# Layer norms whose tiles are turned one by one, with late low parts and a late Newton start

## The reference

```
x = conv block L0 (pooled attention over 64 keys, batch norm, residual)
x = conv block L1 (binary 3x3 and 1x1 convolutions, PReLU)
t = tokens(x)                                    # (8, 256, 64)
t = t + attention_8_heads(layer_norm(t))
t = t + mixture_of_8_experts(layer_norm(t))      # softmax gate, top 2, GELU
t = t + haar_attention(layer_norm(t))
t = t + mixture_of_16_experts(layer_norm(t))     # softmax gate, top 2, SiLU
layer_norm(v) = (v - mean(v)) / sqrt(var(v) + 1e-5), over the 64 channels
```

## Time and profile before

| what | value |
|---|---|
| runs, median (lowest to highest) | 419.47 us (419.42 to 420.14) |
| the profiled execution's own time | 416.06 us |
| its span | 414.3 us |
| its mean granted clock | 0.897 |
| busy: TensorE, VectorE, ScalarE, GpSimd | 350.9, 283.2, 217.5, 189.2 us |

### The profile page before, as it was taken

The page is one execution under the profiler, slowest core; times in us unless marked ns, Lnnn a source line. Parts: engine busy times, 40 slices in busy tenths (PEclk is TensorE's granted clock), DMA queues, the critical chain, the costliest instruction groups (busy, mean ns, idle before and its releaser), DMA issues.

```text
span 414.3 us, 6910 instructions
## 1 busy us (share of the span) xinstructions
PE 350.9 (85%) x2145; PEld 246.1 (59%) x2147; DVE 283.2 (68%) x689; ACT 217.5 (52%) x541; POOL 189.2 (46%) x186
## 2 busy tenths in 40 slices
PE   5666259999999999999769699877258999999996
PEld 1552156787888878887467244374147756666662
DVE  2767876788878878877493587579798545555441
ACT  0534258677677767778547435261315634444441
POOL 4120025545454545545315800122110299999994
PEclk9867559999999999999977789968556999999999
DMA  6916000000000000000000795000000576666521
GB/s 185 235 21 205 0 0 1 2 2 2 2 0 0 0 0 0 0 0 2 1 2 5 288 329 197 2 0 2 1 0 2 193 273 215 222 208 224 204 101 52
DMA packets 17002, 32.87 MB, mean 79 GB/s; under 512 B 6032, under 2 KB 9808, under 8 KB 16976
## 3 DMA queue, kind: packets, MB, share of 16 engines
q1 hardware_dynamic: 16976, 32.55, 23.9%
HBM read 31.83 MB, written 0.72 MB: 79 GB/s over the span
## 4 chain that ended last, share of the span: by engine, by line
PE 61%; DVE 19%; ACT 9%; issue 6%; DMA 3%; POOL 1%; SPq 0%; DVEq 0%; ACTq 0%; POOLq 0%
PE ps L1020 14%; PE ps L1028 7%; PE ps L857 6%; PE ps L884 5%; PE ps L868 5%; PE ps L976 4%; ACT va_vb L619 4%; DVE ln L1504 2%; DVE negmax L1574 2%; PE ps L968 2%; PE ps L807 2%; DMA pT<-gates_row 1%; PE ps L910 1%; PE ps L834 1%; PE ps L833 1%
## 5 line engine op out<-in xcount | busy, mean ns | idle before, releaser
L504 POOL TENSOR_TENSOR va_vb<-va_vb,rowinv 128x512 f32<-128x512 f32 x64 | 67.2, 1050 | 72.1 <-DVE rowinv L1581 72.1
L619 ACT ACTIVATE va_vb<-ps,negmax 128x256 f32<-128x256 f32 x128 | 59.5, 472 | 11.2 <-DVE negmax L1574 10.9
L1020 PE MATMUL ps<-XS,w3hl 128*128 128x512 f32 x256 | 63.4, 406 | 0.7 <-ACT gT L590 0.7
L733 ACT ACTIVATE wy<-ps 128x512 f32<-128x512 f32 x64 | 38.2, 598 | 45.6 <-PE ps L1020 45.6
L1020 PEld LDWEIGHTS ps<-XS,w3hl 128*128 128x128 f32 x256 | 48.6, 193 | 17.2 <-issue 4.9
L1574 DVE TENSOR_REDUCE negmax<-ps 128x2 f32<-128x512 f32 x64 | 44.0, 688 | 7.8 <-PE ps L857 5.6
L857 PE MATMUL ps<-keys_gates,xcur 128*128 128x256 f32 x256 | 47.4, 308 | 2.2 <-DVE keys_gates L1566 2.2
L857 PEld LDWEIGHTS ps<-keys_gates,xcur 128*128 128x128 f32 x256 | 35.1, 193 | 14.8 <-issue 11.5
L868 PE MATMUL ps<-consts,va_vb 128*128 128x128 f32 x256 | 39.5, 277 | 4.2 <-POOL va_vb L504 2.4
L462 POOL TENSOR_TENSOR xn<-T,lnc 128x512 f32<-128x512 f32 x4 | 4.2, 1042 | 74.0 <-DVE lnc L1512 74.0
L868 PEld LDWEIGHTS ps<-consts,va_vb 128*128 128x128 f32 x256 | 29.7, 147 | 9.8 <-POOL va_vb L504 4.8
(11 more groups left out here) (323 smaller groups left out, 727.9 us busy)
## 6 DMA issues: line engine op xcount, KB each, us to landing
pT<-gates_row SPq DMA_DIRECT2D x18, 512.0 KB, 4.8
vproj<-gates_row SPq DMA_DIRECT2D x16, 512.0 KB, 5.4
gate_row_keys<-gates_row SPq DMA_DIRECT2D x14, 512.0 KB, 4.9
early<-in_f_in SPq DMA_DIRECT2D x1, 2048.0 KB, 8.8
consts<-in_consts SPq DMA_DIRECT2D x1, 816.0 KB, 4.9
x<-in_x SPq DMA_DIRECT2D x1, 512.0 KB, 3.7
w2raw<-in_f_in SPq DMA_DIRECT2D x1, 512.0 KB, 3.5
out<-in_f_out SPq DMA_DIRECT2D x1, 512.0 KB
```

Source lines behind the costliest of these rows:

```text
L504: gp.tensor_tensor(prob[:, n % 4], prob[:, n % 4], rowinv[:, n % 4, :].unsqueeze(2).broadcast_to([P, U, N]), ALU.mult).then_inc(S("p_scale ...
L619: ins = act.activation(prob[:, n % 4, u, :], ps[:, 1 + n % 2, u * N:(u + 1) * N], ACT.Exp, bias=negmax[:, n % 4, u:u + 1], accum_out=rowsu ...
L733: act.activation(act_out[:, kk % 2, :], ps[:, 2 * (kk % 3), :], ACT.Silu).then_inc(S("f3_act"), 1)
L1020: mm = pe.matmul(ps[:, 2 * (kk % 3) + w, :], w3hl[:, s, e, w * HID:(w + 1) * HID], XS[:, c * CHUNK:(c + 1) * CHUNK], start=(s == 0), stop= ...
```

## The change

Per chunk there are four transposes of one tile each (64 columns of weights), all into rows 0 to 63 of one bank; one ScalarE copy of 64x512 puts the high part in the upper rows and one VectorE subtraction of 64x512 the low part in the lower. For norm 0 the chunks use banks 0, 5, 4 and 6, which the attention's first steps leave free for a while. In norm 0 VectorE makes only the first chunk's low part and the token copy, then the Newton start and the weight split, and the other three low parts in the attention steps -2, -1 and 0; TensorE waits for the split in step -1 and for the low parts in steps 0 and 1. Both halves of T are copied by ScalarE in norms 0 and 2, and VectorE takes the statistics of the first eight tiles as soon as the first half is there. In the gate the subtraction goes ahead of the comparison and writes to the tile that the exponential then works on in place.

```diff
--- before.py
+++ after.py
@@ -362,25 +362,22 @@
         block = ctx.enter_context(nc.Block())
 
 
+        def norm_bank(n, p):
+
+            return (0, 5, 4, 6)[p] if n == 0 else p
+
+        def chunk_of(stack, p):
+            return stack[:, p * CHUNK:(p + 1) * CHUNK]
+
         def split_high(act, stack, bank, p, signal):
 
-            for odd in range(2):
-                h = slice(C * odd, C * odd + C)
-                act.activation(tiles_of(stack, p, odd)[h], ps[h, bank, 0:2 * P].rearrange("p (t n) -> p t n", n=P),
-                               ACT.Copy).then_inc(S(signal), 1)
+            act.activation(chunk_of(stack, p)[0:C], ps[0:C, bank, :], ACT.Copy).then_inc(S(signal), 1)
 
         def split_low(dve, stack, bank, p, high, so_far, signal):
 
-            for odd in range(2):
-                h, o = slice(C * odd, C * odd + C), slice(C * (1 - odd), C * (1 - odd) + C)
-                dve.wait_ge(S(high), so_far + 2 * p + odd + 1)
-                ins = dve.tensor_tensor(tiles_of(stack, p, odd)[o], ps[h, bank, 0:2 * P].rearrange("p (t n) -> p t n", n=P),
-                                        tiles_of(stack, p, odd)[h].bitcast(F32), ALU.subtract)
-            ins.then_inc(S(signal), 1)
-
-        def tiles_of(stack, p, odd):
-
-            return stack[:, p * CHUNK:(p + 1) * CHUNK].rearrange("p (t o n) -> p t o n", o=2, n=P)[:, :, odd, :]
+            dve.wait_ge(S(high), so_far + p + 1)
+            dve.tensor_tensor(chunk_of(stack, p)[C:P], ps[0:C, bank, :], chunk_of(stack, p)[0:C].bitcast(F32),
+                              ALU.subtract).then_inc(S(signal), 1)
 
         @block.sync
         def _(sp):
@@ -576,12 +573,12 @@
                 act.preload_act_table(table_after)
             for p in range(4):
                 act.wait_ge(S("ln_transposed"), 4 * n + p + 1)
-                split_high(act, XS, p, p, "ln_high")
+                split_high(act, XS, norm_bank(n, p), p, "ln_high")
 
         def gate_act(act, n, first_chunks):
             experts = (EXP2, EXP3)[n]
             act.wait_ge(S("gate_shifted"), n + 1)
-            act.activation(gexp[:, :, 0:experts], logit[:, :, 0:experts],
+            act.activation(gexp[:, :, 0:experts], gexp[:, :, 0:experts],
                            ACT.Exp).then_inc(S("gate_exp"), 1)
             act.preload_act_table((ACT.Gelu, ACT.Silu)[n])
             first_chunks()
@@ -708,9 +705,10 @@
                                ACT.Identity, bias=col[:, 37:38]).then_inc(S("r1_shifted"), 1)
             for p in range(2):
                 positive(p, 2)
-            act.wait_ge(S("x2_transposed"), 1)
-            act.activation(T[:, 0:8, :].rearrange("p t c -> p (t c)"), ps[:, 4, :],
-                           ACT.Copy).then_inc(S("T_act"), 1)
+            for half in range(2):
+                act.wait_ge(S("x2_transposed"), half + 1)
+                act.activation(T[:, 8 * half:8 * half + 8, :].rearrange("p t c -> p (t c)"), ps[:, 4 + half, :],
+                               ACT.Copy).then_inc(S("T_act"), 1)
             ln_act(act, 0, ACT.Exp)
 
             attention_act(act)
@@ -739,8 +737,9 @@
                 gelu(kk)
             act.wait_ge(S("f2_out_chunk"), CHUNKS * EXP2 - 2)
             act.activation(sums[:, 0, :], ps[:, 6, :], ACT.Copy).then_inc(S("f2_sum_act"), 1)
-            act.wait_ge(S("f2_turned"), 1)
-            act.activation(stream_half(0), turned_half(0), ACT.Copy).then_inc(S("T_act"), 2)
+            for half in range(2):
+                act.wait_ge(S("f2_turned"), half + 1)
+                act.activation(stream_half(half), turned_half(half), ACT.Copy).then_inc(S("T_act"), 1)
             ln_act(act, 2)
 
             for half in range(2):
@@ -789,10 +788,8 @@
 
             for p in range(4):
                 pe.wait_ge(S("ln_normalised"), 4 * n + p + 1)
-                for t in range(2):
-                    q = CT * p + 2 * t
-                    mm = pe.transpose(ps[:, p, t * P:(t + 1) * P],
-                                      xn[:, q:q + 2].rearrange("p t c -> p (t c)"), ident)
+                for t in range(CT):
+                    mm = pe.transpose(ps[0:C, norm_bank(n, p), t * P:(t + 1) * P], xn[:, CT * p + t, :], ident)
                 mm.then_inc(S("ln_transposed"), 1)
 
         def gate_pe(pe, n):
@@ -921,6 +918,10 @@
                     keys(j, k + 2)
                 if in_loop:
                     newton_a()
+                if not in_loop and k == -1:
+                    pe.wait_ge(S("qkvw_ready"), 4)
+                if not in_loop and k in (0, 1):
+                    pe.wait_ge(S("ln_low"), k + 3)
                 if there(k):
                     turn(j, 2 * k)
                 if there(k + 1):
@@ -942,7 +943,6 @@
                     products(j, k - 1)
 
             pe.wait_ge(S("fold_split"), 3)
-            pe.wait_ge(S("nsx_ready"), 2)
             pe.sem_inc(S("pv_done"), PAIRS)
             pe.sem_inc(S("out_turned"), G)
             attention_steps(pe, step)
@@ -1472,16 +1472,16 @@
                 dve.wait_ge(S("r1_shifted"), p + 1)
                 norm_and_prelu(p, 2, "conv1_ready", 1, x2, "a2", "b23", "x2_ready")
 
-            dve.wait_ge(S("consts_loaded"), 16)
-            for d in range(2):
-                ins = dve.tensor_copy(eyedup[:, d * C:(d + 1) * C], ident[0:C, 0:C])
-            step(ins)
-            dve.wait_ge(S("ns_norm_done"), 1)
-            step(dve.reciprocal(nsc[:, 1:2], ps[:, 7, C:C + 1]))
-            ts(nsX[:, 2, :], nsAT[:, 0, :], nsc[:, 1:2], None, ALU.mult).then_inc(S("nsx_ready"), 1)
-            ts(nsX[:, 0:2, :], nsA[:].unsqueeze(1).broadcast_to([P, 2, C]), nsc[:, 1:2], None,
-               ALU.mult).then_inc(S("nsx_ready"), 1)
-
+            def newton_start():
+                dve.wait_ge(S("consts_loaded"), 16)
+                for d in range(2):
+                    ins = dve.tensor_copy(eyedup[:, d * C:(d + 1) * C], ident[0:C, 0:C])
+                step(ins)
+                dve.wait_ge(S("ns_norm_done"), 1)
+                step(dve.reciprocal(nsc[:, 1:2], ps[:, 7, C:C + 1]))
+                ts(nsX[:, 2, :], nsAT[:, 0, :], nsc[:, 1:2], None, ALU.mult).then_inc(S("nsx_ready"), 1)
+                ts(nsX[:, 0:2, :], nsA[:].unsqueeze(1).broadcast_to([P, 2, C]), nsc[:, 1:2], None,
+                   ALU.mult).then_inc(S("nsx_ready"), 1)
 
             def query_or_key(part, h):
                 return qkvw[:, part, 0:P].rearrange("p (a h c) -> p a h c", a=2, h=2)[:, :, h, :]
@@ -1493,14 +1493,12 @@
                                        (qkvw[:, 0, P:192], qkvw[:, 1, P:192], ps[:, 7, 0:C])):
                     step(dve.tensor_copy(high, raw))
                     tt(low, raw, high.bitcast(F32), ALU.subtract).then_inc(S("qkvw_ready"), 2)
-            split_projections()
-            dve.wait_ge(S("x2_transposed"), 2)
-            step(dve.tensor_copy(T[:, 8:16, :].rearrange("p t c -> p (t c)"), ps[:, 5, :]))
-            dve.wait_ge(S("T_act"), 1)
 
             def layer_norm(n, after_first=None):
 
                 for q in range(TILES):
+                    if n % 2 == 0 and q % 8 == 0:
+                        dve.wait_ge(S("T_act"), n + q // 8 + 1)
                     ins = dve.bn_stats(ln6[:, q, :], T[:, q, :])
                 step(ins)
 
@@ -1520,10 +1518,15 @@
                     if p == 2:
                         dve.wait_ge(S("ln_centred"), n + 1)
                     tt(xn[:, q], xn[:, q], wide(lnc[:, 7, q], t=CT), ALU.mult).then_inc(S("ln_normalised"), 1)
-                for p in range(4):
-                    split_low(dve, XS, p, p, "ln_high", 8 * n, "ln_low")
-                    if p == 0 and after_first:
-                        after_first()
+                if after_first:
+                    low(n, 0)
+                    after_first()
+                else:
+                    for p in range(4):
+                        low(n, p)
+
+            def low(n, p):
+                split_low(dve, XS, norm_bank(n, p), p, "ln_high", 4 * n, "ln_low")
 
             def gate(n):
 
@@ -1538,8 +1541,8 @@
                     for q in range(8 * half, 8 * half + 8):
                         ins = dve.max(top8[:, q, :], lg[:, q, :])
                 step(ins)
+                tt(ge, lg, wide(top8[:, :, 0], experts), ALU.subtract).then_inc(S("gate_shifted"), 1)
                 step(tt(gs, lg, wide(top8[:, :, 1], experts), ALU.is_ge))
-                tt(lg, lg, wide(top8[:, :, 0], experts), ALU.subtract).then_inc(S("gate_shifted"), 1)
                 dve.wait_ge(S("gate_exp"), n + 1)
                 step(tt(gs, ge, gs, ALU.mult))
 
@@ -1559,7 +1562,12 @@
                 dve.tensor_copy(xcur[:, m % 2, :].rearrange("p (u n) -> p u n", u=U).unsqueeze(1),
                                 src[:, at, :, m % 2, :]).then_inc(S("xcur_ready"), 1)
 
-            layer_norm(0, after_first=lambda: tokens(0, 0))
+            def while_first_keys():
+                tokens(0, 0)
+                newton_start()
+                split_projections()
+
```

(6 more changed lines are left out.)

## The result

| what | before | after |
|---|---|---|
| median of the runs | 419.45 us (416.30 to 420.14, 4 runs) | 413.03 us (412.62 to 413.48, 4 runs) |
| profiled execution, span | 416.06, 414.3 | 413.05, 411.2 |
| mean granted clock | 0.897 | 0.913 |
| busy TensorE, VectorE, ScalarE, GpSimd | 350.9, 283.2, 217.5, 189.2 | 349.5, 278.7, 214.6, 188.5 |

The ratio is 0.9874 (95% interval 0.9834 to 0.9914). Ratios and intervals use only the runs within 1.5% of the fastest run of the same kernel; medians are of all runs. The two profiled executions differ by 3.0 only. These are two questions: why 3.0 and not 2.1, and why the medians differ by twice what the traces do.

What follows compares the result with a forecast made beforehand. It took serial engine hand-overs in the four norms and a final GpSimd queue as the bound. Gains of 0.6 + 0.27 + 0.85 + 0.40 = 2.1 us gave a median of 417.4 us, range 415.4 to 419.0.

Steps and rivals of the forecast that it cites:

- the sum against the traced execution: Whole kernel: gains of 2.1 us taken off the profiled execution of 416.06, giving 413.96.
- the carry from that execution to the median: Whole kernel: the profiled execution's 3.4 us under the median was carried over in microseconds, giving a median of 417.4.
- Norm 0's entry: Start of norm 0: ScalarE's second copy of T and the later Newton start and split end the statistics 1.63 us sooner.
- the first rival: Norm 0: VectorE does not wait for GpSimd's bias adds; norm 0 gives 1.33, median 416.6 us, chance 0.20.
- the value taken: Norm 0, before the keys' low part: the identity copy hangs on GpSimd's adds; low part at 57.2, gain 1.3 us.
- its lower end: Norm 0, same place: the token copy also loses to GpSimd's second add; block ends at 57.4, gain 1.05 us.
- the bound of 0.42: Norm 0, first chunk: four 64-column transposes cost at most 0.42 us more than two of 128; 0.2 was taken.
- The 0.67 for the late low parts: First attention steps: chunk 2's low part costs 0.47 us and chunk 3's 0.20, with chunk 1's free.
- with no gap at half clock: Behind norms 1 and 2: gate matmuls (3.60 us) and projections (6.56) run unbroken at half clock, so later low-part savings give nothing.
- a rival at 0.10: TensorE's granted clock: less idling and more transposes delay its fall, saving 1.35 us at the projections; median 416.0, chance 0.10.
- the last stage is a GpSimd queue: Last stage: GpSimd's 64 products of 1.28 us, 82 in all, set the end, so bringing gate 1 forward brings it forward.
- Slower rival: First attention steps: breaks from low parts delay full clock, losing 0.41 per microsecond; at 9 us 421.1, chance 0.06.

Runs made afterwards that it cites:

- after_lows_early: The changed kernel with all four of norm 0's low parts made before the attention: 415.76 us, ratio 0.9929 to the kernel before.
- after_pairs: The changed kernel with the old pair transposes and two 64x256 copies and subtractions per chunk: 416.33 us, ratio 0.994 to the kernel before.
- pairs_twice: after_pairs with each pair transposed twice, the second time over the first: 416.86 us, ratio 0.9986 to the kernel before.
- turns_only: The kernel before with only the four one-tile transposes and single 64x512 copy and subtraction per chunk, no late low parts: 418.6 us, ratio 0.9999.
- before_again: The kernel before, unchanged, run again: 418.82 us over 12 runs, ratio 0.9985.
- gate_only: The kernel before with only the gate's subtraction moved ahead of the comparison and the exponential in place: 418.63 us, ratio 0.9986.
- before_keep_f2: The kernel before with 13 unused matmuls on TensorE while it waits for gate 0's rows: 417.35 us, ratio 0.9964.
- after_keep_gate1: The changed kernel with 8 unused matmuls on TensorE while gate 1 is worked out: 412.54 us, ratio 0.9876 to the kernel before.
- before_keep: The kernel before with unused matmuls in TensorE's idle stretches ahead of the transposes of norms 0, 1 and 3: 421.2 us, ratio 1.0046.
- after_delay2: The changed kernel with ten one-column VectorE copies added behind norm 0's statistics: 416.71 us, ratio 0.9961 to the kernel before.

## Why the prediction was right and wrong

The median came out at 413.0 where 417.4 was forecast. Of these 4.4 us the sum against the traced execution is 0.9 short (413.96 forecast, 413.05 measured), and the carry from that execution to the median 3.4 too high. That the sum is as near as this is in part luck: at gate 1 the lead was 4.87 for 2.1, and the last stage took 1.8 of it back.

**Right, by its steps.** Norm 0's entry: the statistics ended at 48.88 (the second eight are 1.11 from 47.77), 1.6 earlier than before when the late x2 is taken off, as forecast (1.63). One 64x512 copy takes 0.59, one low part 0.68 (0.60 and 0.69 taken). Norm 2's entry gained 0.98 (0.91). The gates' exponential starts at the subtraction's end. Late low parts are worth having (after_lows_early). VectorE does lose to GpSimd's bias adds, against the first rival.

**A bound, not the value taken.** The held instruction was the token copy (1.24), not the identity copy; the prediction had this as its lower end, 1.05 of gain (58.50 less its own 57.35 is 1.15), and 1.1 came. It came by another wait: the moved block had ended at 57.72, and the keys' low part waited for ScalarE's high part, which had itself hung on the late token copy. after_pairs shows that the value taken (identity copies 1.36) was right for another issue time, 0.5 us sooner. The first chunk's four turns took 0.37 longer than the two (1.10 for 0.73 from their start to ScalarE's copy), near the bound of 0.42 and not the 0.2 taken. The 0.67 for the late low parts did not show: from the keys' low part to norm 1's statistics the lead grew by 0.19, as the clock was full 5.9 us sooner. In after_pairs, at the clock of before and with low parts of 0.86, that stretch takes 150.2 for 148.9, 1.3 lost.

**First failed step: "with no gap at half clock".** Norm 1, norm 2 and both gates were costed at the clock of before; that the clock would change was a rival at 0.10 and is what happened. The first scores, gate 0 (3.60 to 2.34), the projections (6.56 to 3.79) and gate 1 (3.61 to 2.35) carry the lead at gate 1's exponential from a forecast 2.1 to 4.87: gate 0 brings 1.36 between the norm's statistics and the exponential where 0.27 was forecast, gate 1 1.38 for 0.40. In the trace of after_pairs, which has the rest of the order, all these places ran at half, so the turns are needed for it; they are not all, as pairs_twice, with as many, still ran gate 0 at half. Of the projections' 2.77 only 0.55 reached norm 3's statistics: the lead was 4.51 where the next matmuls (L1063) begin, 282.03 and 277.52, and 3.49 behind them and L1068, as the clock was at half there for 4.9 us (to 282.4) and not 2.9 (to 284.9). The rival's low chance leaned on a rule: the Trainium skill (TensorE: Matmul & The Clock Gate, Part 4) says that the full clock does not engage for transposes. The trace disagrees: pairs_twice adds transposes alone to after_pairs, and the full clock comes at 56.8 instead of 63.8; turns_only has it at 57.8 for 63.0. The measurement decides. The rival's own sum (1.35 for the projections) left out both gates, which carry most of it. Full clock at these places is not enough by itself: turns_only and pairs_twice had it at gate 1 and in part or all of the projections, and were no faster.

**Second: the carry to the median.** The sum stood against an execution of 416.06, and the 3.4 us to the median went over as a constant. They are no constant: before's runs spread over 415.1 to 422.5, and two traces show the half clock lasting longer in the Haar stage (before_again, 2.0 us) or behind gate 0 (gate_only, 3.9 us); the changed kernel's runs spread over 1.9 us. 3.0 of the fall of 6.4 is in the two traces; the other 3.4 is that the changed kernel's runs stay near its traced one. Against the larger groups of runs (418.87 and 413.24) it is 2.6. Why they stay there is open. The turns have a part in it, as after_pairs spreads over 6.5 us, and before_keep_f2, which fills one of the two places, has a median 1.6 lower (ratio 0.9932 to 0.9996).

**Third: "the last stage is a GpSimd queue".** GpSimd's 64 products at 1.28 nearly fill it, but the chain that ended last, in the trace of before too, runs over TensorE's hidden and output matmuls and meets GpSimd once, for 0.97 us. So GpSimd starting 4.43 sooner was not worth 4.43. The 56 hidden matmuls took 2.76 more at half clock, 0.97 came back from that one wait, and the lead fell from 4.8 to 3.1. after_keep_gate1 takes this back in its trace: 13.38 and 1.6 us.

**Slower rival.** Breaks in the first steps did not delay the full clock in the changed kernel (57.1), but the mechanism exists: after_lows_early, pairs_twice, turns_only, before_keep and after_delay2 all show the clock fall back between 55 and 67 us.
